# Laying the first six attention steps between the V tiles, and a new instruction order in the drain of a fused two-layer kernel

## The reference, cut to what matters

```python
# layer 0
q, k, v = x @ w_q, x @ w_k, x @ w_v               # 16 heads of 64
allowed = same 64-token segment | (|i-j| % 4 == 0 and 0 < |i-j| <= 256)
attn = softmax(q @ k.T * scaling + mask);  x += (attn @ v) @ w_o
h = silu(fp4(x) @ fp4(w_gate).T) * (fp4(x) @ fp4(w_up).T);  x += fp4(h) @ fp4(w_down).T
# layer 1
q, k, v, a, g = split(x @ in_proj_w.T, 5)
state = a * state + k * v                          # over the tokens
x = mix(x, (gate * (q * state) + (1 - gate) * v) @ out_proj_w.T)
x = mix(x, silu(rms(x) @ fc_w.T) @ proj_w.T)
x = x + sigmoid(xr @ W_r.T) * (relu(xk @ W_k.T) ** 2 @ W_v.T)
```

## Time and profile before

| | us |
|---|---|
| time, median of 3 (lowest, highest) | 542.6 (541.2, 543.77) |
| the profiled execution: its time | 544.28 |
| its span, first to last instruction | 542.3 |
| busy in the span: PE, DVE, ACT, POOL | 466.6, 418.9, 354.1, 310.1 |

### The profile page before, as it was taken

One profiled execution on the slowest core, in us unless ns is written; L12 is line 12 of the kernel. 1 busy time (PEld: TensorE's weight loads), 2 busy tenths in 40 slices (PEclk: granted clock), 3 DMA queues, 4 the chain that ended last, 5 costly groups with the idle time before them and its releaser, 6 DMA issues.

```text
span 542.3 us, 17269 instructions
## 1 busy us (share of the span) xinstructions
PE 466.6 (86%) x6418; PEld 357.7 (66%) x6418; DVE 418.9 (77%) x1337; ACT 354.1 (65%) x1021; POOL 310.1 (57%) x497
## 2 busy tenths in 40 slices
PE   0898569999999999999999999987748778749996
PEld 0774458878777877878787888765326455437685
DVE  3774359978999999999998786958889694795243
ACT  3444458687767777676777777646435598676855
POOL 4030258685766767575777574575365787883221
PEclk9999969999999999999999999989959798878999
DMA  6267640354444344443555454320000000000002
GB/s 194 115 235 264 171 99 5 60 119 94 84 84 94 74 92 76 82 99 73 122 123 111 103 118 83 69 61 1 0 1 1 0 0 2 0 0 2 0 2 77
DMA packets 136099, 40.53 MB, mean 75 GB/s; under 512 B 104976, under 2 KB 131024, under 8 KB 136016
## 3 DMA queue, kind: packets, MB, share of 16 engines
q1 hardware_dynamic: 135440, 38.38, 30.7%
q10 hardware_dynamic: 576, 1.05, 0.6%
HBM read 29.44 MB, written 9.96 MB: 73 GB/s over the span
## 4 chain that ended last, share of the span: by engine, by line
PE 49%; DVE 27%; ACT 7%; issue 6%; DMA 6%; POOL 3%; SPq 2%; ACTq 0%; DVEq 0%; POOLq 0%
PE psum L449 6%; PE psum L409 5%; PE psum L1122 5%; PE psum L1117 4%; DVE pband L691 4%; DVE pt L752 3%; PE psum L469 3%; PE psum L483 3%; PE psum L390 3%; PE psum L495 3%; PE psum L480 2%; ACT pband L551 2%; DMA w_rows_dram<-st 2%; PE psum L1113 2%; PE psum L392 2%
## 5 line engine op out<-in xcount | busy, mean ns | idle before, releaser
L929 POOL TENSOR_SCALAR pband<-pband,fac 128x192 f32<-128x192 f32 x256 | 103.9, 425 | 96.8 <-DVE fac L743 95.1
L551 ACT ACTIVATE pband<-pband,st 128x192 f32<-128x192 f32 x256 | 113.2, 448 | 0.0
L691 DVE CUSTOM_DVE_ANT_0 pband<-psum,band_mask 128x192 f32<-128x192 f32 x256 | 76.0, 353 | 1.7 <-PE psum L409 1.6
L409 PE MATMUL psum<-keys,q_class 64*64 64x192 f32 (+2 forms) x1536 | 67.2, 279 | 0.0
L911 POOL COPY keys<-k_rows 128x512 f32<-128x512 f32 x32 | 36.4, 1137 | 45.2 <-ACT k_rows L583 29.9
L449 PEld LDWEIGHTS psum<-ident,pband 128*128 128x128 f32 x384 | 46.0, 143 | 24.0 <-issue 16.9
L409 PEld LDWEIGHTS psum<-keys,q_class 64*64 64x64 f32 x1536 | 58.5, 136 | 1.9 <-issue 1.6
L449 PE MATMUL psum<-ident,pband 128*128 128x128 f32 x384 | 54.4, 277 | 4.3 <-DVE pt L752 3.7
L551 ACT ACTIVATION_READ_ACCUMULATOR pband<-pband,st 128x1 f32 x256 | 49.3, 193 | 0.0
L752 DVE COPY pt<-psum 128x512 f32<-128x512 f32 x64 | 43.8, 685 | 6.8 <-PE psum L449 6.6
L1117 PE MATMUL psum<-xt,arena 128*128 128x512 f32 x72 | 40.1, 682 | 3.7 <-ACT xt L1359 1.6
(11 more groups left out here) (208 smaller groups left out, 1149.0 us busy)
## 6 DMA issues: line engine op xcount, KB each, us to landing
v_rows_dram<-arena SPq DMA_DIRECT2D x32, 256.0 KB, 2.3
v_both<-v_rows_dram SPq DMA_DIRECT2D x32, 256.0 KB, 3.7
v_seg<-v_rows_dram SPq DMA_DIRECT2D x64, 128.0 KB, 3.5
v_side<-v_rows_dram SPq DMA_DIRECT2D x96, 64.0 KB, 2.5
w_rows_dram<-st SPq DMA_DIRECT2D x64, 8.0 KB, 2.9
st<-w_rows_dram SPq DMA_DIRECT2D x64, 8.0 KB, 2.4
arena<-_attn_hidden_states_dram SPq DMA_DIRECT2D x4, 256.0 KB, 4.7
out_dram<-x SPq DMA_DIRECT2D x4, 256.0 KB, 2.3
```

The costliest lines, as they stand in the source:

```text
L409: return pe.matmul(bank[2 * r + head][rows, at:at + y.shape[1]], x, y, start=True, stop=True, skip_group_check=True)
L551: act.activation(x, x, ACT.Exp, bias=mine[:, head:head + 1], scale=-1.0, accum_out=mine[:, 2 + head:3 + head]).then_inc(s_exp, 1)
L691: dve.tensor_tensor_reduce(pband[:, G % P_SLOTS, c, head, :], bank[2 * r + head][:, at:at + BAND], band_mask[:, (0, 1, 1, 2)[w], SEG * (1 ...
L929: pool.tensor_scalar(x, x, fac[:, F % 2, 1, c, head:head + 1], 1.0, ALU.mult, ALU.mult).then_inc(s_scaled, 1)
```

## The change

`FIRST_STEP` goes from 3 to 6: the hand-written lists now hold steps 0 to 5 up to the first turns of step 0, laid between the 32 tiles of V, and the loop runs from t = 6. The tiles go half by half (all 16 token tiles of heads 0 to 7, then those of heads 8 to 15). The exchange is split into `send_statistics` and `fetch_statistics`, so that SP can issue stores of V between them. The copies of the queries go from DVE to ACT in the run-in. `RAW_STEP` and `QUANT_STEP` move two steps back, and so do the splits of the second half of the q/k weights (`split_qk(1, ...)`, on DVE t = 5, 6 before and 7, 8 now). In the drain every engine has the same steps in another order, with group 0 first throughout. No arithmetic is added or removed.

```diff
@@
-    FIRST_STEP = 3
+    FIRST_STEP = 6
...
-    RAW_STEP, QUANT_STEP, ROW_STEP, PLAIN_STEP = 4, 10, 20, 24
+    RAW_STEP, QUANT_STEP, ROW_STEP, PLAIN_STEP = 6, 12, 20, 24
...
-        return TW * (i // (2 * TW)) + i % TW, i // TW % 2
+        return i % NT, i // NT
...
-    occupants = [(x, who) for x in range(FIRST_STEP) for who in ("key", "query")]
+    occupants = [(0, "key")]
+    for x in range(1, FIRST_STEP):
+        occupants += [(x, "key"), (x - 1, "query")]
+    occupants.append((FIRST_STEP - 1, "query"))
@@ SP
-            store_v(3, 1)
-            exchange(0)
-            load_v(0, 3)
-            sp.dma_start(wo[:, :, :], w_o.rearrange("(p q) d -> q p d", q=P)).then_inc(s_wo, 16)
+            store_v(0); store_v(1); store_v(2); store_v(3); store_v(4); store_v(5); load_own(0, 0); store_v(6)
+            store_v(7); store_v(8); load_own(0, 1); load_sides(0, 1); store_v(9); store_v(10); store_v(11)
+            store_v(12); store_v(13); load_own(0, 2); load_sides(0, 2); send_statistics(0); store_v(14); store_v(15)
+            store_v(16); store_v(17); store_v(18); store_v(19); fetch_statistics(0); store_v(20); store_v(21)
+            send_statistics(1); store_v(22); load_own(0, 3); load_sides(0, 3); load_wo(); fetch_statistics(1)
+            store_v(23); store_v(24); store_v(25); store_v(26); store_v(27); store_v(28); store_v(29); store_v(30)
+            store_v(31)
@@ PE
-            turn_rows(0); values(0); values(1); values(2); turn_rows(1); project(0, 1); values(3); values(4)
...
-            values(26); values(27); values(28); values(29); values(30); values(31)
+            turn_rows(0); values(0); values(1); turn_rows(1); values(2); project(0, 1); values(3); project(1, 1)
+            values(4); values(5); turn_rows(2); project(0, 0); values(6); values(7); turn_rows(3); values(8)
+            scores(0, 0); values(9); project(2, 1); values(10); project(1, 0); values(11); values(12); scores(0, 1)
+            values(13); project(3, 1); values(14); values(15); scores(1, 0); project(2, 0); values(16); values(17)
+            project(4, 1); values(18); values(19); scores(1, 1); scores(2, 0); values(20); values(21); project(3, 0)
+            values(22); values(23); scores(2, 1); values(24); values(25); project(5, 1); values(26); values(27)
+            project(4, 0); values(28); values(29); scores(3, 0); values(30); values(31); project(5, 0); turn(0, 0)
+            scores(3, 1); turn(0, 1); turn(0, 2)
@@ DVE, end of the run-in
+            seg_sums(2); differences(1); take_values(31); even_turned(0, 0); factors(1); band_max(3, 0)
@@ PE, drain (a part)
-            pg(2); pa(2); trx(0); t4(3); trx(1); pq(2); pv(3); pk(3); pg(3); pa(3); pq(3); qq(2); op(0); qq(3); op(1)
-            trx(2); t5(1); fc0(1); trx(3); t5(0); fc1(1); fc2(1); fc0(0); op(2); fc3(1); op(3); pr(1); fc1(0); fc2(0)
+            dn(2); t4(1); pv(1); pk(1); t3a(3); pg(1); trx(0); pa(1); t3b(3); t4(2); pq(1); op(0); pv(2); pk(2); dn(3)
+            pg(2); pa(2); qq(1); pq(2); qq(2); t5(0); fc0(0); trx(1); fc1(0); t4(3); fc2(0); pv(3); op(1); pk(3)
```

More of the change, by code:

```diff
@@ L248, in load_x, with store_v @@
                     "(n q) d -> q n d", q=P)).then_inc(s_x[part_], 16)
[L250 to L255, removed]
+            def store_v(i):
+                n, half = v_tile(i)
+                sp.wait_ge(s_vev[i % 2], i // 2 + 1)
+                sp.dma_start(v_rows[P * n:P * (n + 1), HALF_HD * half:HALF_HD * (half + 1)],
+                             v_sb[:, i % V_SLOTS, :]).then_inc(s_vst[i % V_SLOTS], 16)
             def stored(half, w):
-                for i in range(2 * TW * w + TW * half, 2 * TW * w + TW * (half + 1)):
+                for i in range(NT * half + TW * w, NT * half + TW * (w + 1)):
                     sp.wait_ge(s_vst[i % V_SLOTS], 16 * (i // V_SLOTS + 1))
@@ L281, in load_sides, with load_wo, send_statistics @@
                                          "(x c) f -> x c f", c=DIL)).then_inc(s_v[w], 16)
[L283 to L289, removed]
+            def load_wo():
+                sp.dma_start(wo[:, :, :], w_o.rearrange("(p q) d -> q p d", q=P)).then_inc(s_wo, 16)
+            def send_statistics(F):
                 seg, band = place_of_stats(F, 0), place_of_stats(F, 1)
@@ L440, in turn @@
                     pe.wait_ge(s_segscaled, U + 1)
+                if U == 0 and b < 2:
+                    pe.wait_ge(s_vev[odd], V_TILES // 2)
                 wait(pe, s_pt[odd], e)
@@ new lines, in _ @@
+            turn_weights(6); turn(30, 2); turn_weights(7); turn(30, 1); weigh(29, 0); weigh(29, 1); weigh(29, 2)
+            weigh(29, 3); turn(30, 3); output(29); weigh(30, 0); turn(31, 0); t1(1); weigh(30, 1); weigh(30, 2)
+            weigh(30, 3); turn(31, 2); turn(31, 1); output(30); turn(31, 3); weigh(31, 0); weigh(31, 1); weigh(31, 2)
+            t1(2); weigh(31, 3); t2(0); output(31); gu0(0); t1(3); gu1(0); gu2(0); t2(1); gu0(1); gu3(0); gu1(1)
+            gu2(1); t2(3); gu3(1); gu0(3); t2(2); gu0(2); gu1(2); gu2(2); t3a(0); gu3(2); gu1(3); t3b(0); dn(0)
@@ L869, in _ @@
                 seg_sums(t - 2)
[L870 to L872 removed]
+                if t in (7, 8):
+                    split_qk(1, 8 - t)
+                if t == 8:
                     dve.wait_ge(s_wlo, 4)
@@ new lines, in _ @@
+            clear(); factors(30); seg_sums(31); accumulate(28); x1(0); even_turned(30, 0); bn0(0); ag0(0)
+            even_turned(30, 2); differences(31); factors(31); qx0(0); qx1(0); qx2(0); qx3(0); accumulate(29)
+            even_turned(31, 0); x1(1); bn0(1); ag0(1); qx5(0); even_turned(31, 2); accumulate(30); qx7(0); qx8(0)
+            qx0(1); qx1(1); qx2(1); qx3(1); x1(2); bn0(2); ag0(2); qx5(1); accumulate(31); qx7(1); x1(3); bn0(3)
+            hm0(0); ag0(3); qx8(1); qx0(2); qx1(2); hm1(0); qa0(0); qa1(0); qa2(0); qa3(0); qx0(3); qx1(3); hm2(0)
```

203 lines of the change are left out of this document (90 added, 113 removed), and 8 rows, old and new, of the table STEPS.

## The result

| | before | after |
|---|---|---|
| time, median (lowest, highest), us | 543.2 (541.2, 545.2) | 526.4 (525.2, 529.2) |
| ratio, 95% interval | | 0.9698 (0.9645 to 0.9752) |
| the profiled execution: time, span | 544.28, 542.3 | 525.24, 523.5 |

The change takes 16.8 us (13.5 to 19.3 by the interval). I forecast 24, and a range from 510 to 531. The time lies in the range, but 0.4 us beyond the forecast's own range (511 to 526): the mechanism came and its size was too large.

The account below looks back on a forecast made before the run. It saw holes at both ends of PE's span, with chains between engines. Run-in and loop 15 (15.8 less 0.9) plus drain 9 made 24 us off 544.28: 520.3, median near 519; own range 511 to 526, eight in ten 510 to 531.

Parts of the forecast that it names:

- The bound and the floor: Holes at both ends of the span; in the run-in, PE without waits reaches step 6's keys at 59.6 us, 21.3 sooner.
- The mark: Start of the keys of step 6, the new loop's first step: from 80.89 us to 65.1, 15.8 us sooner.
- The wait of `differences(1)`: Run-in, DVE ahead of the copy of tile 31, waiting for the statistics of step 1: 1.5 us, between 0 and 3.
- The unplaced waits: Run-in: exponentials and maxima holding ACT and DVE, late stores making copies wait for ring slots: 4 us together, 1 to 10.
- the run-in's gain is real but later steps wait for statistics: Rival: each of the first two loop steps waits 2 us, time 523 us; counted with the forecast's 74%.
- The work given back in the loop: Splits of the second half of w_q and w_k on DVE now both in full steps: 0.9 us lost, 0 to 1.9.
- The drain: End of the kernel: 9 us gained, from PE waits 6.3, the `gu3(3)` wait 2 and the clock 1; bounds -3 to 14.
- what is saved is PE time that stood empty: Drain: DVE and POOL chains stay as long, so only PE's waits of 5.49 and 0.78 us go, 6.3 us.
- The signs: Observations to show it right (PE at least 17 busy per 20 us, first SiLU product 18 us sooner) or wrong (long engine waits).
- the drain gives nothing: Rival: DVE and POOL get in each other's way in the drain, its gain of 9 us is lost: 528 us, chance 12%.
- Run-in bound by DMAs or copies: Rival: the two unplaced waits take 14 us, not 4; step 6's keys at 75, time 529 us, chance 9%.
- SP's queue as the way to a slower kernel: Rival: each of 65 run-in DMAs costs 1.18 us to issue; step 6's keys at 95.2, time 549 us, chance 3%.

Follow-up runs that it names:

- the earlier sending: New kernel with the statistics of step 2 sent behind the store of tile 26 and fetched behind that of tile 29, not behind tile 31: 524.0 us.
- the run-in alone: New run-in and loop with all drain lists of the kernel before: 534.1 us against 544.6, ratio 0.9813.
- the last experiment: New kernel with the quantisation of the rows of group 3 ahead of that of the hidden rows of group 0 in the drain: 527.3 us.
- the drain alone: Run-in and loop of the kernel before with the new drain: 537.9 us against 544.6, ratio 0.9868.
- the old tile order: New kernel with V's tiles window by window, both halves, and loads behind needed stores: 534.8 us; with window 3's loads behind the fetch of step 2: 524.1 us.
- the kernel with SP re-ordered: New kernel with SP's run-in list re-ordered: stores 14, 15 before window 2's loads, statistics sent once they exist, w_o last: ratio 0.9615, median 526.5 us.
- the ring edit: New kernel with the stores of tiles 14 and 15 ahead of window 2's loads, and tile 16's ahead of its side loads: 525.8 us, ratio 0.9654.
- the queries on DVE: New kernel with the copies of the queries of steps 0 to 5 on DVE instead of ACT: 526.3 us, ratio 0.9684.

## Why the prediction was right in kind and too large

- **The bound and the floor.** Two readings were loose: the sixth slice of the earlier trace rows is a 6, not an 8, and the four engines at two thirds each are busy 77, 68, 63 and 54%. The holes at both ends were where the time was. The mark moved from 81.5 (mean of the two profiles with the old run-in) to 67.2 (mean of the five whose code is that of the new run-in up to there), 14.3 us where I had 15.8.
- **The wait of `differences(1)`.** Taken at 1.5 us, measured 1.37 at 65.01. Right in place; the size is in part luck, since the other profiles with that order have from none to 1.28 us there. The fit of the Trainium skill (DMA: Bandwidth & Descriptors, Anatomy of one DMA), with 2.0 us and almost nothing for 8 KB, is made for another issuing path and is not borne out here: from the fetch, issued at 61.38, to DVE's row at 65.01 it took 3.6 us.
- **The unplaced waits.** Taken at 4 us with the ring of slots as the third of their causes. The ring was the largest in most profiles: DVE stood 2.29 to 6.05 us for it in the profiles with that order, and PE's pauses ahead of tiles 24 to 26 follow. Taking it away gained 1 us at most, since the statistics of step 0 are late behind it.
- **The step that failed: "the run-in's gain is real but later steps wait for statistics".** I left this out of the sum, as a case inside the range. It is shown: DVE waits 3.2 to 3.9 us for step 2, one step behind my mark. The mark counted as saved a wait of 2.77 us ahead of it that had only moved behind it. From the keys of step 6 to those of step 7 the kernels with the new run-in unchanged take 9.7 to 11.0 us, the old 8.9: 1.3 us on the mean of four. With the earlier sending it is 7.9, 2.3 us under that mean.
- **The work given back in the loop.** The splits, taken at 0.9, measured 1.0 to 1.1, at step 10. Some 0.6 us more went between steps 12 and 31 (178.3 against 177.7), but all kernels together spread from 177.5 to 178.8 there, so it is not shown.
- **The sum of the first half.** 14.3 - 1.3 - 1.1 leaves 11.9; the marks of step 31 say 11.7 (314.2 less 302.5), and the time of the run-in alone 10, where I had 15.
- **The drain.** Taken at 9 and measured at 7 (7.9 by the rest behind the keys of step 31: 230.0, the mean of two, less 222.1, the mean of twelve). The size was near, its parts were not. Behind the keys of step 31 PE's idle time fell by 5.3 us (43.9, the mean of two, to 38.6, the mean of eleven, without the last experiment), where 6.3 + 2 stood, and its busy time by 2.7 (186.1 to 183.5), where I had put 1 for the clock. The first pair alone says 5.0 and 5.0, but the same code profiled again was busy 185.2 us there, not 180.9: about half of that fall is scatter. The waits of 5.49, 6.70 and 4.10 us went, a wait of 6.29 came. The step "what is saved is PE time that stood empty", priced wait by wait, is not how it works: DVE is busy 25.7 of the 28 us from 372 to 400, and PE's waits there move when one is taken away. That DVE sets the pace there is argued from this, not shown by an edit that gives DVE less to do. The order itself did more than I forecast: counted from the keys of step 31, `x3_0` comes 22 us sooner by the same means, and the first product of the SiLU network 22 us in the first pair, where I had 19, and only 7 to 8 of it reach the end.
- **The signs.** Two of the right ones failed narrowly: from 60 to 80 us PE is busy 16.69, not 17, and the first product comes 27.7 us behind the end of the quantisation where it came 41.9 behind it, 14 sooner and not 18 (the quantisation ends at 444.88 and 428.51, by these rows of the kernel before and the new one; the row of 444.81 that I took for it is the `x2` behind it). Two of the wrong ones came: DVE's 4.93 us for a store, and PE's 6.29 us for POOL.

```profile
443.20 1.68 DVE L1529 SCALAR_TENSOR_TENSOR area<-area 128x704 f32<-128x704 f32 x2
```

```profile
426.82 1.69 DVE L1531 SCALAR_TENSOR_TENSOR area<-area 128x704 f32<-128x704 f32 x2
```

- **The rivals.** That the drain gives nothing is refuted by the drain alone; DVE is busy 160.0 us behind the keys of step 31, and was 160.5, so it is held up no more than before. "Run-in bound by DMAs or copies" was right in part: the mark did not go to 75, but the wait was of that family, with the queue's order as the cause. SP's queue as the way to a slower kernel did not come; its price of 1.18 us for an issue was far off (nine stores in 7.18 us, 0.80 each). But part of the missing microseconds is in the queue (sending step 2 sooner brings step 7 forward), and a poor order of it costs some 10 us (534.8 against 524.1, both with the old tile order).

## What to carry to other kernels

A mark that is to measure a gain must lie behind every wait that can move; follow the same kind of wait one step past it, in the order of the queue that feeds it. In a queue that issues in order, whatever waits for a landing holds up all behind it (11.18 us of waiting in the worst case here): list for each entry when it is ready and when it is due, and put the loads due last behind the small transfers due first. Where several engines are half to three quarters busy, don't sum the waits of one of them: a wait taken away shows up elsewhere unless the engine behind it gets less to do.

## What the runs showed of the hardware

- The same subtraction on DVE (128x512, two inputs) took 0.68 and 0.98 us in the new kernel, 1.87 before, and 2.29 in the kernel with SP re-ordered (the row below), where POOL multiplied and copied beside it from 96.35 to 100.1. In the new kernel the 0.68 fell into a pause of POOL. The Trainium skill (SBUF — State Buffer, Who interferes with whom) states that an operation of VectorE with two inputs in SBUF and one of GpSimd that reads SBUF keep each other out. The trace agrees: the operation of 2.29 us ends at 100.65, 0.55 us behind POOL's last. So the price of a moved operation depends on where it lands:

```profile
98.36 2.29 DVE L788 SCALAR_TENSOR_TENSOR w_lo<-arena,w_hi 128x512 fp32r<-128x512 f32 x1
```

- A wait of PE can be followed by a lower clock, which lengthens the step further, but the length of the wait doesn't say whether it is. In the profile of the new kernel the granted clock was 0.81 from 75 to 80 us, with the wait of 2.71 us, and 0.85 in the next 5 us, with PE busy all the time; step 7 took 10.64 us. In its second profile, with a wait of 1.56 us, it was 1.00 in both, and the step took 9.28. That looks like a rule, and two other kernels break it: with the ring edit the wait was 2.72 us, the clock stayed at 1.00 and the step took 9.26; with the queries on DVE the wait was 1.75 us, the clock fell to 0.66 behind it and the step took 10.90. What decides is open. The stretches, in this order:

```profile
75.00:80.00 5.00, 2.29 (x9) 1.38 (x7) 3.15 (x16) 1.68 (x4) 1.35 (x4) 0.81 0.20 8
80.00:85.00 5.00, 5.00 (x77) 4.13 (x78) 4.34 (x17) 4.89 (x18) 5.00 (x8) 0.85 0.01 3
```

```profile
75.00:80.00 5.00, 3.52 (x29) 2.59 (x30) 4.51 (x19) 3.66 (x12) 2.75 (x6) 1.00 0.14 6
80.00:85.00 5.00, 5.00 (x152) 4.43 (x151) 4.83 (x19) 4.36 (x15) 3.66 (x6) 1.00 0.08 7
```

```profile
75.00:80.00 5.00, 3.52 (x29) 2.59 (x30) 4.51 (x19) 3.67 (x12) 2.75 (x6) 1.00 0.07 3
80.00:85.00 5.00, 5.00 (x152) 4.44 (x150) 4.83 (x19) 4.36 (x15) 3.66 (x6) 1.00 0.09 7
```

```profile
75.00:80.00 5.00, 3.25 (x40) 2.31 (x34) 2.39 (x12) 1.93 (x6) 0.59 (x2) 1.00 0.15 7
80.00:85.00 5.00, 5.00 (x40) 3.67 (x41) 4.49 (x19) 4.27 (x16) 5.00 (x10) 0.66 0.07 3
```
